# Moving a layer norm's second half to the turn that made its sum, and fetching expert rows one pair earlier, in a decoder layer on one core

## The reference

```python
x = x + _L0_attn_ref(_layernorm(x), ...)              # 16-head attention + relu MLP
x = x + _L0_xattn_ref(_layernorm(x), ctx, ctx, ...)   # 8-head cross-attention
#   q_enh = _layer_norm(query + attn_out, ln1_g, ln1_b)
#   return _layer_norm(q_enh + ffn, ln2_g, ln2_b)     # the "second layer norm"
x = x + _L0_ffn_ref(_layernorm(x), ...)
#   xn = _rms_norm(x, scale);  ids = argmin(dist2(xn, centroids))
#   y = (a * silu(g)) @ down_w[ids], with (a, g) = xn @ up_w[ids]
#   return y + skip
```

## Time and profile before

| | us |
|---|---|
| median of 3 runs | 1496.47 (1495.56 to 1498.79) |
| the profiled execution, its own time | 1503.02 |
| its span, first to last instruction | 1501.3 |
| loop turns, start to start | 65.5 each |
| experts, first up product to the end | 1205.11 to 1501.3 |
| TensorE busy | 1287.7 (86%) |
| VectorE, ScalarE, GpSimd busy | 813.5, 554.3, 429.2 |

### The profile page before, as it was taken

One profiled execution on the slowest core, in us unless ns is written; L12 is line 12 of the kernel. 1 busy time (PEld: TensorE's weight loads), 2 busy tenths in 40 slices (PEclk: granted clock), 3 DMA queues, 4 the chain that ended last, 5 costly groups with the idle time before them and its releaser, 6 DMA issues.

```text
span 1501.3 us, 27047 instructions
## 1 busy us (share of the span) xinstructions
PE 1287.7 (86%) x8806; PEld 933.9 (62%) x8807; DVE 813.5 (54%) x2080; ACT 554.3 (37%) x1179; POOL 429.2 (29%) x657
## 2 busy tenths in 40 slices
PE   3187999999999999999999999999997288888887
PEld 1055767777676777767677776767775145555544
DVE  3245566765768667576767757686654611211111
ACT  1224353543535354363635445363531022121211
POOL 2110203231322324132232413223222333434342
PEclk9578999999999999999999999999999589999998
DMA  6910000000000000000000000000063011111111
GB/s 90 288 31 15 1 15 11 20 28 0 28 0 28 4 24 23 5 28 0 28 0 28 18 10 28 0 28 8 16 230 134 14 50 51 53 49 49 48 59 25
DMA packets 44483, 58.77 MB, mean 39 GB/s; under 512 B 6549, under 2 KB 38111, under 8 KB 44192
## 3 DMA queue, kind: packets, MB, share of 16 engines
q1 hardware_dynamic: 38832, 43.87, 10.1%
q0 software_dynamic: 5616, 14.43, 3.3%
HBM read 42.54 MB, written 16.66 MB: 39 GB/s over the span
## 4 chain that ended last, share of the span: by engine, by line
PE 54%; DVE 16%; issue 11%; POOL 7%; ACT 5%; DMA 5%; SPq 3%; POOLq 0%; DVEq 0%; ACTq 0%
PE bank L1302 49%; DMA shared<-rows_x,shared 4%; POOL shared L883 3%; ACT shared L700 2%; PE bank L1464 2%; DVE a_p L1121 2%; POOL out_rows L901 2%; ACT a_p L695 1%; DVE a_sq L1081 1%; SPq L552 1%; DVE shared L998 1%; PE bank L1323 1%; POOL shared L778 1%; DVE shared L953 1%; DVE shared L1090 1%
## 5 line engine op out<-in xcount | busy, mean ns | idle before, releaser
L1302 PE MATMUL bank<-shared 128*128 128x256 f32 (+4 forms) x2242 | 449.9, 381 | 35.3 <-POOL shared L878 11.3
L1302 PEld LDWEIGHTS bank<-shared 128*128 128x128 f32 (+2 forms) x2242 | 319.4, 174 | 115.9 <-issue 32.4
L1121 DVE TENSOR_TENSOR a_p<-a_p,eb 128x385 f32<-128x385 f32 x256 | 125.9, 555 | 75.7 <-ACT a_p L695 75.7
L1302 PE MATMUL bank<-up,shared 128*128 x312 | 139.6, 601 | 0.9 <-issue 0.9
L845 POOL TENSOR_SCALAR a_rz<-a_ms 128x2 f32<-128x2 f32 x16 | 3.1, 193 | 418.8 <-ACT a_sq L706 418.8
L695 ACT ACTIVATE a_p<-bank 128x385 f32<-128x385 f32 x256 | 105.2, 503 | 41.6 <-PE bank L1302 41.5
L1302 PE MATMUL bank<-a_xnT,w 128*128 128x256 f32 x512 | 114.7, 382 | 1.4 <-ACT a_xnT L612 1.4
L1302 PE MATMUL bank<-w,a_hT 128*128 128x256 f32 x512 | 113.1, 379 | 0.0
L1302 PEld LDWEIGHTS bank<-a_xnT,w 128*128 128x128 f32 x512 | 96.0, 190 | 18.0 <-issue 3.4
L1302 PEld LDWEIGHTS bank<-w,a_hT 128*128 128x128 f32 x512 | 97.3, 190 | 13.2
L961 DVE TENSOR_SCALAR shared<-shared 128x256 f32<-128x256 f32 x128 | 67.5, 578 | 68.3 <-POOL shared L778 62.2
(11 more groups left out here) (197 smaller groups left out, 2128.9 us busy)
## 6 DMA issues: line engine op xcount, KB each, us to landing
up<-in_L_ffn_up_w SPq DMA_DIRECT2D x8, 1024.0 KB, 13.8
x_in<-in_x SPq DMA_DIRECT2D x16, 256.0 KB, 2.7
shared<-in_ctx SPq DMA_DIRECT2D x16, 256.0 KB, 2.9
rows_x<-shared SPq DMA_DIRECT2D x16, 256.0 KB, 2.2
rows_skip<-shared SPq DMA_DIRECT2D x16, 256.0 KB, 2.3
down<-in_L_ffn_down_w SPq DMA_DIRECT2D x8, 512.0 KB, 12.3
toep<-a_hT SPq DMA_DIRECT2D x1, 3072.0 KB, 33.3
eb<-toep SPq DMA_DIRECT2D x2, 1024.0 KB, 7.4
```

Source lines behind the costliest of these rows:

```text
L1121: tt(a_p[:, n_ % NPA], a_p[:, n_ % NPA], eb[:, n_], ALU.mult).then_inc(sig["a_p"], 1)
L1302: return mm(out, lhsT=lhsT, rhs=rhs, start=first, stop=last, **kw)
```

## The change

Three things are moved. In the first part, `c_norm`, the scaling (gain), the sum `c_x2`, its statistics and `c_norms` are made at the end of the turn in which D made `b_f`, for batch `dd`; at the head of the next turn only `c_xs` and `c_xl` are left, now ahead of the sum of squares. In the experts' part, two more input gathers are issued before the first pair, and in every step the gather is that of the pair after next. And TensorE's order inside a pair is interleaved, with ScalarE's following it.

```diff
@@ tile_steps @@
-        body(0, 2, 2)
-        with eng.Fori(0, PAIRS - 2) as k:
-            body(k + 1, 2, 2)
-        body(PAIRS - 1, 2, TILES_MAX - 2 * PAIRS)
+        body(0, 2, 2, 2)
+        with eng.Fori(0, PAIRS - 3) as k:
+            body(k + 1, 2, 2, 2)
+        body(PAIRS - 2, 2, 2, TILES_MAX - 2 * PAIRS)
+        body(PAIRS - 1, 2, TILES_MAX - 2 * PAIRS, 0)
...
@@ ScalarE, step @@
                 nc.scalar.activation(m_sg[:, u], bank[3 + 2 * u][:], ACT.Silu)...
+                after_tile(act, "m_ht", k, u)
+                copy(m_hT[:, u]...)
             for u in range(nxt):
                 transposed(k + 1, u)
-            for u in range(n):
-                after_tile(act, "m_ht", k, u)
-                copy(m_hT[:, u]...)
@@ GpSimd, turn @@
-            if Cc:
-                after(pool, "c_mv", c)
-                layer(c_mv, c_rs, "c_norm", c, 1e-5)
...
-            if Cc:
-                after(pool, "c_mv2", c)
-                layer_then_rms(c_mv2, c_sc, "c_norms", c, 1e-5)
...
+            if Dd:
+                after(pool, "c_mv", dd)
+                layer(c_mv, c_rs, "c_norm", dd, 1e-5)
+                after(pool, "c_mv2", dd)
+                layer_then_rms(c_mv2, c_sc, "c_norms", dd, 1e-5)
             if A:
                 after(pool, "b_mv", a)
                 layer(b_mv, b_rs, "b_norm", a, 1e-5)
@@ GpSimd, experts @@
+        for u in range(2):
+            after_tile(pool, "m_x", 0, u)
+            gather(m_in, rows_x, sorted_row[:, 2 + u:3 + u], "m_loaded", u)
-            for u in range(nxt):
-                after_tile(pool, "m_x", k, u)
+            for u in range(nxt2):
+                after_tile(pool, "m_x", k + 1, u)
                 after_tile(pool, "m_row", k, u)
                 gather(m_in, rows_x, m_row[:, 0, u], "m_loaded", u)
@@ VectorE, experts @@
-            for u in range(nxt):
-                after_tile(dve, "m_loaded", k, u)
-                ts(m_row[:, 0, u], of_tile(3, 2 * k + 2 + u), ...)
             for u in range(n):
                 ... m_h ...
+            for u in range(nxt2):
+                after_tile(dve, "m_loaded", k + 1, u)
+                ts(m_row[:, 0, u], of_tile(3, 2 * k + 4 + u), ...)
@@ TensorE, experts @@
+            up_half(0, 0)
+            up_half(0, 1).then_inc(mig[0]["m_up"], 1)
+            up_half(1, 1)
+            turn_hidden(0)
+            up_half(1, 0).then_inc(mig[1]["m_up"], 1)
+            down_tile(0)
+            turn_hidden(1)
+            for u in range(nxt):
+                transpose_in(k + 1, u)
+            down_tile(1)
```

More of the change, by code:

```diff
@@ L722, in transposed, with step @@
             copy(m_xT[:, u].rearrange("p c s -> p (c s)"), bank[u][:, 0:C * P]).then_inc(mig[u]["m_xT"], 1)
-        def step(k, n, nxt):
+        def step(k, n, nxt, nxt2):
             for u in range(n):
@@ L995, in turn @@
             if Cc:
[L996 to L1004, removed]
-                                             ALU.add).then_inc(sig["c_x2"], 1)
+                after(dve, "c_norms", c)
+                shifted(c_rows[:, :, 0:D], c_x2, c_mv2, c_sc[:, 6], "c_xs")
+                shifted(c_n, c_x2, c_mv2, c_sc[:, 1], "c_xl")
             def nearest():
@@ L1082, in turn @@
                        bc(a_rn[:, t], D0), ALU.mult).then_inc(e_sem(f"A.qk{t}"), 1)
-            if Cc:
-                after(dve, "c_x2", c)
-                stats(c_x2, c_st, c_mv2, "c_stats2", "c_mv2", c)
             def maxima(jobs):
@@ L1104, in turn @@
                 scale_rows(w0v, 0, s_v, V_LOADED)
-            if Cc:
-                after(dve, "c_norms", c)
-                shifted(c_rows[:, :, 0:D], c_x2, c_mv2, c_sc[:, 6], "c_xs")
-                shifted(c_n, c_x2, c_mv2, c_sc[:, 1], "c_xl")
             if A:
@@ L1159, in turn @@
                 shifted(a_xl, x_in, a_mv, a_sc[:, 1], "a_xl")
+            if Dd:
+                after(dve, "c_norm", dd)
+                for t in range(T):
+                    dve.scalar_tensor_tensor(b_f[:, t], b_f[:, t], c_mv[:, t, 0:1], vecs[:, G2], ALU.subtract,
+                                             ALU.mult).then_inc(sig["c_gain"], 1)
+                after(dve, "c_stored", dd - 1)
+                after(dve, "x1_kept2", dd)
+                for t in range(T):
+                    after(dve, "c_gain", dd, t + 1)
+                    dve.scalar_tensor_tensor(c_x2[:, t], b_f[:, t], c_rs[:, 1, t:t + 1], x1_keep2[:, t], ALU.mult,
+                                             ALU.add).then_inc(sig["c_x2"], 1)
+                after(dve, "c_x2", dd)
+                stats(c_x2, c_st, c_mv2, "c_stats2", "c_mv2", dd)
             if A:
@@ L1599, in step, with up_half, turn_hidden @@
                 expert.append(pe.value_load(at, min_val=0, max_val=E - 1))
-            for u in range(n):
-                after_tile(pe, "m_xT", k, u)
-                after_tile(pe, "m_h", k, u, 0)
-                if u == 0:
-                    after_tile(pe, "m_hT", k, 1, 0)
-                else:
-                    after_tile(pe, "m_out", k, 1, 0)
-                for half in range(2):
-                    for c in range(C):
-                        w = up[:, bass.ds(expert[u], 1), c, half * EH:(half + 1) * EH]
-                        ins = product(bank[2 + 2 * u + half][:], m_xT[:, u, c], w.rearrange("p o n -> p (o n)"),
-                                      c == 0, c == C - 1)
-                ins.then_inc(mig[u]["m_up"], 1)
-            for u in range(nxt):
-                transpose_in(k + 1, u)
-            for u in range(n):
+            def up_half(u, half):
+                for c in range(C):
+                    w = up[:, bass.ds(expert[u], 1), c, half * EH:(half + 1) * EH]
+                    ins = product(bank[2 + 2 * u + half][:], m_xT[:, u, c], w.rearrange("p o n -> p (o n)"),
+                                  c == 0, c == C - 1)
+                return ins
+            def turn_hidden(u):
                 after_tile(pe, "m_h", k, u)
@@ L1622, in step, with down_tile @@
                 ins.then_inc(mig[u]["m_ht"], 1)
-            for u in range(n):
+            def down_tile(u):
                 after_tile(pe, "m_hT", k, u)
```

20 lines of the change are left out of this document (15 added, 5 removed).

## The result

The changed kernel takes 1465.34 us (median, 1462.45 to 1468.59; before 1497.63 beside it), a ratio of 0.9774 with a 95% interval of 0.9752 to 0.9797. A second series gave 0.9767 (0.9738 to 0.9796). It is faster, as forecast, but by 32.3 us where 46.4 (1496.5 to 1450.1) was forecast, and 1.3 us above the range's upper end. (The before of this series is 1.2 us above the 1496.47 that the forecast started from; 0.9774 of 1496.47 is 1462.6, inside the range of 1438 to 1464 and outside the forecast's own 1443 to 1457.) Its profiled execution took 1462.45 us (span 1460.5) against the 1503.02 of before: 40.6 less, where the sum of steps said 49.6.

A forecast was written before the change was run, and what follows sets the result against it. TensorE, busiest, was taken to wait on late gathers behind GpSimd's queue and on VectorE's maxima. -45.9 - 6.5 + 1.8 + 1.0 = -49.6 from 1503.0 gives 1453.4, less half of 6.5: 1450.1; range 1443 to 1457 (wider 1438 to 1464).

The forecast's parts named there:

- The pair of tiles: Experts: a pair falls from 14.90 to 12.35 us, 45.9 us less over 18 pairs.
- Subtracting the three waits: Experts' pair: taking TensorE's idle 0.84, 0.88 and 0.33 us from 14.37 leaves 12.32 us.
- a wait of about 0.36 us stays: Experts' pair: TensorE still waits about 0.36 us ahead of the second tile's down products.
- 0.15 us margins: Experts' pair: issued work covers the hand-overs from ups to hidden transposes with 0.15 us left over, for each tile.
- The turn: Head of a loop turn: score maxima start 0.5 us earlier, 6.5 us less over 13 turns.
- The port lock: Turn's head: VectorE's `b_xl` and shifts stand behind GpSimd's instructions; if the shifts don't, 15.6 us gained instead of 6.5.
- The drain: Pipeline's end: 1.8 us lost in BDC waiting for `b_xl`, 1.0 us lost in DC.
- DC's: Drain part DC: `c_rows` starts at 1151.1 in place of 1150.15, behind `d_q` twice and `x1_keep2`; 1.0 us lost.
- The level: Whole kernel: half of the 6.5 us between profiled execution and median is taken off, 1453.4 to 1450.1.
- hand-overs bind: Experts: hidden transposes and last copy cost 0.3 us more each, pair 13.2, or low clock stays; 1457 to 1470; 16 in 100.
- The slower case: Experts: GpSimd's queue becomes the limit at 2.6 us a transfer, pair 15.6, time 1505; 4 in 100.
- No contention at the turn's head: Loop turn's head: gain 1.2 us a turn, no BDC loss; 1439, down to 1430; 11 in 100.

The follow-up runs named there:

- e5: Changed kernel with TensorE's register load of the second tile's expert moved behind the first tile's up products: 1455.76 us, ratio 0.9703.
- e7: Changed kernel with GpSimd's `d_q`, `x1_keep2` moved behind VectorE's `a_lo_q`, and `c_rows` ahead of `a_lo_k`, waiting for the last shift: 1446.45 us, ratio 0.9641.
- e8: Changed kernel with the edits of e7 and e5 together: 1434.69 us, ratio 0.9550 to the kernel before.
- e9: Changed kernel with one more, unused register load of an expert's number at the head of every pair on TensorE's queue: 1477.52 us, ratio 0.9838.
- e4: Changed kernel with interleaved orders kept but gathers issued where the kernel before issues them, one pair ahead of use: 1470.97 us, ratio 0.9805.

## Why the prediction came out as it did

- **The pair of tiles** is the term that failed. "Subtracting the three waits" and "a wait of about 0.36 us stays" were right, and so were the 0.15 us margins: no hidden transpose waits. But the sum was made of TensorE's instructions alone. It left out that the queue between two pairs has a branch and two register loads, which the old order hid behind most of sixteen downs and the new one has to hide behind eight. It measured 13.12 in place of 12.35; with that removed (e5) the pair is 12.37. The term was 45.9 and came to 33.4 in the profiles (296.2 - 262.8). For work that no engine row shows it did not ask what hides it and what it costs without that cover.
- **The turn** came out at -8.6 us to the last A.out for -6.5, by other steps, 0.8 of it ahead of the loop; that the sums lie so near is luck. The ordinary turn gained 0.22, not 0.5. The shifts waited, 4.34 us for six where about 4.9 was forecast, and the sum of squares began 0.1 us earlier after A.out (7.70 to 7.60), not 0.5 later; with the statistics' 1.0 gone the maxima came 1.1 us earlier. But `c_rows` on `a_lo_q` took 0.91 of that back: from the first transposes of A's heads to the products behind them it is 1.96 us before (659.39 to 661.35) and 2.87 in the changed kernel. The prediction followed GpSimd's `d_q` and `x1_keep2` and stopped there; that `c_rows`, ready earlier, follows `a_lo_k` without a break was not looked at. The rest is the low clock of four turns, 5.6 us, which the prediction looked for among the experts only.
- **The port lock.** The prediction took it that the tensor_scalar shifts stand behind GpSimd "since both instruction kinds would have the cover of the same rows". They do: 4.34 us for six beside GpSimd, 2.03 away from it (e7). In a loop turn the chain of `b_qh` covered it; in BDC it is the wait. The Trainium skill ("SBUF — State Buffer", "Who interferes with whom") has them blocked only in a two-port mode; the measurement agrees with that if they run in it.
- **The drain.** BDC's wait is 1.78 us where about 2 was forecast, 1.6 more than the earlier trace rows for +1.8. From the last A.out to the first up it is 107.89 us against 106.74, +1.15 for a forecast 2.8. But the second profile of before has 103.9 there and e8 103.4, so a term of 1 us, DC's among them, is not to be read from it.
- **The level.** Half of the profiled execution's gap to the median, 3.25 us, was taken off. It went the other way: the changed kernel's profiled execution is 2.9 below its median. So 15.2 us of miss (1465.3 - 1450.1) are 9.0 of the steps (12.5 of the experts, less 2.1 of the turns and 1.7 of the drain, and 0.3 of rounding and of what lies outside the span) and 6.2 of the level. Taking off half the gap was a guess at its cause; the profiled execution of before had a start like the changed kernel's, and one of the longer routing parts.
- **Rivals.** The nearest, "hand-overs bind", gave a pair of 13.2 and 1457 to 1470, and the time fell there, by another mechanism: no hand-over binds. The slower case found nothing: transfers stay at 0.95 to 1.01 us. "No contention at the turn's head" put the gain at 1.2 a turn. At the maxima the changed kernel had 1.11 of it (the wait of 2.15 fell to 1.04) in spite of the contention, since the chain of `b_qh` covers it; e7, with the contention gone, has 1.20 there and 1.37 in the turn (65.49 - 64.12).

## What to carry to other kernels

Count what a loop's end costs on the engine's queue, the branch and each register load (about 0.7 us here), and see how much issued work is left when the queue's last wait ends: an order in which that wait ends late in the body uncovers it. Two edits that cure the same wait do not add; run each alone, since one may be the better kernel without the other. Before work is moved on GpSimd, list everything large that it will start earlier and lay it against VectorE's instructions of that time, and see what else VectorE waits for there: contention under another wait costs nothing.

## What the runs showed of the hardware

- A register load that nothing covers on TensorE's queue cost 0.75 us of a pair (the second, e5 against the changed kernel) and 0.67 (the third, e9); the load itself is recorded at 0.30 and up to 0.55 in e4, a register step at 0.15.
- A compare-and-branch is 0.21 us on TensorE's queue.
- VectorE's tensor_scalar of 128x256 f32, 0.34 us apart alone, stands up to a whole GpSimd instruction of 1.09 to 1.24 us.
- The granted clock fell some 2 us after a wait of 2.15 us ended at four of eleven loop turns, every third one and the same in three profiles; behind the same wait of the others it stayed at 1.00.
